# Norm reductions on two PSUM regions, and a broadcast moved by one step, in the attention pairs of a macaron block

## What is computed

```python
# x: (8, 2048, 1024); 16 heads of 64; d_ff 4096, rank 256
x = x + 0.5 * ffn(layernorm(x))          # gelu(P @ V1 + b1) with P = y @ U1, then @ U2 @ V2
x = x + attn(layernorm(x))
x = x + 0.5 * ffn(layernorm(x))

def attn(y):
    q, k, v = (einsum('bpm,hmd->bphd', y, W) + b for W, b in ...)
    logits = einsum('bqhd,bkhd->bhqk', q, k) / sqrt(64)   # causal mask
    return einsum('bqhd,hdm->bqm', einsum('bhqk,bkhd->bqhd', softmax(logits), v), O_w) + O_b
```

## Time and profile before

| | us |
|---|---|
| median of 2 runs | 2237.23 (2233.7 to 2240.76) |
| profiled execution, time | 2229.34 |
| profiled execution, span of the slowest core (core 4) | 2227.6 |
| TensorE busy in that span | 1510.3 (68%) |
| VectorE busy | 569.8 (26%) |
| ScalarE busy | 553.7 (25%) |
| GpSimd busy | 95.0 (4%) |

### The profile page before, as it was taken

One profiled execution on the slowest core, in us unless ns is written; L12 is line 12 of the kernel. 1 busy time (PEld: TensorE's weight loads), 2 busy tenths in 40 slices (PEclk: granted clock), 3 DMA queues, 4 the chain that ended last, 5 costly groups with the idle time before them and its releaser, 6 DMA issues. The chain is left out here.

```text
span 2227.6 us, 17635 instructions; the slowest of 8 cores (2185.7 to 2227.6 us)
## 1 busy us (share of the span) xinstructions
PE 1510.3 (68%) x5571; PEld 415.2 (19%) x5640; DVE 569.8 (26%) x911; ACT 553.7 (25%) x609; POOL 95.0 (4%) x108
## 2 busy tenths in 40 slices
PE   3089997167537586686675876865767578189994
PEld 0022221022112121121121211211211122022221
DVE  3322214442302313114023131131321125312211
ACT  1222231100022232332322323333234201232221
POOL 0100000000100000000000000000100000100000
PEclk9588997588767767576677576767876589599986
DMA  7400000101030100100101101001000102300003
GB/s 223 118 1 1 1 1 14 62 29 62 6 67 0 31 17 10 38 1 10 38 1 29 19 10 38 1 10 29 1 19 0 45 31 71 119 1 1 0 1 151
DMA packets 63652, 72.66 MB, mean 33 GB/s; under 512 B 20390, under 2 KB 51254, under 8 KB 61516
## 3 DMA queue, kind: packets, MB, share of 16 engines
q1 hardware_dynamic: 63564, 71.54, 11.2%
HBM read 50.49 MB, written 12.58 MB: 28 GB/s over the span
## 5 line engine op out<-in xcount | busy, mean ns | idle before, releaser
L668 ACT ACTIVATE pt<-p_big 128x1024 bf16<-128x1024 f32 (+3 forms) x320 | 286.3, 895 | 646.4 <-PE p_big L635 397.0
L629 PE MATMUL p_big<-qgA,kgA 65*128 65x512 bf16 (+3 forms) x320 | 143.8, 449 | 200.8 <-DMA kgB<-u_row 98.9
L531 ACT ACTIVATE hb<-p_big 128x1024 bf16<-128x1024 f32 x128 | 130.7, 1023 | 308.6 <-PE p_big L454 306.7
L452 PE MATMUL p_big<-pb,v1b 128*128 128x512 bf16 x498 | 156.1, 394 | 16.0 <-DVE pb L489 14.9
L590 PE MATMUL p_big<-pt,v_pair 128*64 128x512 bf16 (+3 forms) x320 | 149.9, 469 | 0.0
L593 PE MATMUL p_big<-pt,v_pair 128*64 128x512 bf16 (+3 forms) x320 | 149.5, 467 | 0.0
L635 PE MATMUL p_big<-qgB,kgB 65*128 65x512 bf16 (+3 forms) x320 | 148.6, 464 | 0.0
L586 PE MATMUL p_big<-pt,ones_bf 128*1 128x512 bf16 (+3 forms) x320 | 145.1, 453 | 0.0
L582 PE MATMUL p_big<-pt,ones_bf 128*1 128x512 bf16 (+3 forms) x320 | 138.4, 433 | 0.7
L462 PE MATMUL p_big<-hb,u2b 128*128 128x512 bf16 x502 | 134.4, 389 | 5.9 <-ACT hb L531 4.7
L893 PE MATMUL p_big<-nsq,ones2b 128*1 128x512 bf16 x128 | 51.9, 547 | 81.7 <-DVE u_sc L944 60.0
(11 more groups left out here) (140 smaller groups left out, 1570.9 us busy)
## 6 DMA issues: line engine op xcount, KB each, us to landing
wstage<-u SPq DMA_DIRECT2D x40, 256.0 KB, 4.7
wstage<-v SPq DMA_DIRECT2D x40, 256.0 KB, 4.2
x<-xT SPq DMA_DIRECT2D x8, 1024.0 KB
outT<-x SPq DMA_DIRECT2D x8, 1024.0 KB, 11.0
wstage<-vw SPq DMA_DIRECT2D x16, 256.0 KB
vscr<-vb_s SPq DMA_DIRECT2D x32, 128.0 KB
wst<-qw SPq DMA_DIRECT2D x8, 512.0 KB
wst<-kw SPq DMA_DIRECT2D x8, 512.0 KB
```

Source lines behind the costliest of these rows:

```text
L452: tensor.matmul(psl, v1b[:, rc, 128 * fc:128 * (fc + 1)], pb[:, c % 2, rc, :], start=(rc == 0), stop=False)
L531: ACT.inc(scalar.activation(hb[:, 2 * (fp % 2):2 * (fp % 2) + 2, :], psl.rearrange("p (a b) -> p a b", a=2), AF.Gelu_apprx_tanh))
L629: mm = tensor.matmul(p_big[:, 0:w], kgA[:, ksl], qgA[:, lo:hi], start=True, stop=not first)
L668: ch["XA"].inc(scalar.activation(pt[:, :, i % 2, 0:w], p_big[:, 0:1024].rearrange("p (a b) -> p a b", a=2)[:, :, 0:w], AF.Exp))
```

## The change

1. `emit_bc(c)`, for c = 0, 1, 2, is called at step IC[c]+4 in place of IC[c]+3: 13, 22 and 27.
2. On VectorE, rdbcp(2) and evac(2) stand between round 0 and round 1 of the reductions, no longer behind round 1.
3. Each lane has two rows of PSUM, used by even and odd rounds. Odd rounds use p_big2 columns 0 to 511 (where the projections were) for three lanes, and row 0 of p_big2 columns 1024 to 1535 (where query block 2's output was) for lane (1, 1). So round 1 no longer waits for reductions but for the last copy of the projections (WS) or for evac(2) (DR + 3), and rounds 2 and 3 wait for the reductions of round j-2.
4. The norm matmul (1, 1, 1) is moved from step 26 to step 28.

The number of instructions stays the same on every engine, but for waits.

```diff
@@ the steps of a pair, TensorE @@
-                        c_bc = ICR.get(i - 3)
+                        c_bc = ICR.get(i - 4)
@@ VectorE's order @@
                         aux["dve_red"](vector, 0, 0)
                         aux["dve_red"](vector, 1, 0)
+                    rdbcp(2); evac(2)
+                    if aux:
                         aux["dve_red"](vector, 0, 1)
                         aux["dve_red"](vector, 1, 1)
-                    rdbcp(2); evac(2)
@@ emit_attn_aux_begin @@
-            def nrm_region(which, h):
+            def nrm_region(which, h, j):
                 lane = 2 * which + h
                 if lane < 3:
-                    return p_big2, 32 * lane, 512
-                return p_big, 64, 1024
+                    return p_big2, 32 * lane, (512 if j % 2 == 0 else 0)
+                return (p_big, 64, 1024) if j % 2 == 0 else (p_big2, 0, 1024)
@@ mk_nrm @@
-                    if j >= 1:
-                        tensor.wait_ge(ch["UC"].h, uc_after[(which, j - 1)])
-                    pb, base, coff = nrm_region(which, h)
+                    if in_pair and (which, h) == (1, 1) and j == 1:
+                        tensor.wait_ge(ch["DR"].h, dr0 + 3)
+                    if j == 1 and 2 * which + h < 3:
+                        tensor.wait_ge(ch["WS"].h, ws0 + 10)
+                    if j >= 2:
+                        tensor.wait_ge(ch["UC"].h, uc_after[(which, j - 2)])
+                    pb, base, coff = nrm_region(which, h, j)
@@ the list of items @@
-                items.append((max(26, 24 + 2 * j), ("nrm", 1, 1, j)))
+                items.append((max(26 if j == 0 else 28, 24 + 2 * j), ("nrm", 1, 1, j)))
```

## The result

The changed kernel takes 2184.0 us (median; 2168.4 to 2207.5) beside 2240.2 us for the kernel before, a ratio of 0.9736 (95% interval 0.9698 to 0.9774): 59 us, or 2.6%, faster. The ratio leaves out two runs of the changed kernel (2201.8 and 2207.5 us) that were in a second, slower state with a lower granted clock on one die, so the two medians as they stand differ by 56 us. The forecast was 2162 us in a range of 2140 to 2190. So the direction was right and the time lies in the range, but about 15 us of the 74.5 us forecast are missing. Averaged over repeated runs (59 of the kernel before, 10 of the changed one), the mean span over the eight cores fell from 2223.5 to 2160.1 us and the slowest core's from 2241.4 to 2179.9 us, so it is no effect of one core.

The account below looks back on a forecast made before the run. The prediction took TensorE, with its waits on VectorE's reductions and rdbcp, to bound the attention pairs. Gains of 52 + 8.5 + 11 + 3 = 74.5 us took 2229.3 to 2154.8, or 2162 by the median; range 2140 to 2190.

Parts of the forecast that it names:

- the forecast's own part of it: Whole kernel: the span of times given to the main forecast, 2150 to 2175 us, at a chance of 0.53.
- rival A: TensorE stays at the low clock from step 22 to 39: gain 55 us, 2182 by the median; chance 0.22.
- The stalls and their order: Steps 25 to 28: the 6.95 us wait goes, rdbcp(2)'s falls to about 1 us, nrm(1,1,1) isn't late.
- Where the stall goes: hilo(2) to ScalarE's tail: VectorE's chain becomes the bound, 9.4 us sooner in five pairs, 12.5 in pair 1.
- 59.5 + 8.5: hilo(2) to the tail: 59.5 us gained over pairs 0 to 5, and 8.5 in pair 6.
- The low clock behind the new wait: Steps 36 to 39: TensorE idles behind ScalarE's wait, then runs low, costing 1.5 us in five pairs, 7.5.
- emit_bc: Broadcast one step later covers TensorE's wait for hilo: 1.4 us in 8 pairs, 11, plus 3 in pair 7.
- the clock part: Clock assumptions, to be judged wrong if pairs' stretches before hilo(2) changed by more than 3 us.
- The rule on the clock: From step 25: sustained work would bring the high clock once the 7 us gap goes; the profile row needn't agree.
- rival B: In the pairs, the clock comes up early: gain 98 us, 2131, by the median 2139; chance 0.13.

Follow-up runs that it names:

- e1_bc_only: The kernel before with emit_bc one step later and nothing else: 2242.8 us, ratio 0.9994.
- e7_no_bc_move: The changed kernel with emit_bc back at its old steps (12, 21, 26): 2206.6 us, ratio 0.9823 to the kernel before.

## Why the prediction was right, and where it was not

*The time.* The range held, but the forecast's own part of it, 2150 to 2175, did not: 2184 is the figure of rival A (2182). Its mechanism is not what happened. Rival A had TensorE at the low clock from step 22 to 39 and no wait of ScalarE; in pair 2 the clock was 1.00 from 1028 to 1044, and ScalarE waited in 47 of the 48 pairs 0 to 5 of all cores. Only in pair 5 of core 0 did it not. So that the time is A's is chance, and the mechanism below is the forecast's.

*The stalls and their order.* Right. The waits of 6.95 and 1.25 us went, rdbcp's fell to 1.02, nrm(1, 1, 1) was issued before it was needed, and nothing waited for evac(2).

*Where the stall goes.* Right, and to the microsecond: 27.6 us from hilo(2) to the tail was forecast, 27.3 to 28.7 was measured in pairs 0 to 5 over all cores, with a ScalarE wait of 3.4 to 4.8 us in all but one of them (forecast 2 to 6), and none in pair 6, which took 23.6 on the slowest core (25 taken, 22.9 the lower bound for TensorE). Summed over pairs 0 to 6 this stretch fell by 68.3 us against 59.5 + 8.5 = 68 in the sum.

*The low clock behind the new wait.* The right mechanism, sized too small: 1.5 us a pair in five pairs was taken, and 2.2 measured in most of six (tail to hilo(3) 13.25 in place of 11.03). The term had steps 36 to 39 dearer by at most 0.61 each and by less in the narrow ones; in pair 0 of the slowest core, against pair 2 of the kernel before, step 36 took 0.70 more than at the high clock, step 37 0.81, step 38 0.60, and from step 39 on 0.56, less 0.45 at the tail itself. On the mean over cores 11.3 us in place of 7.5.

*emit_bc.* For c = 0 it gave 1.7 us a pair where 1.4 was taken, and pair 7 in all 4.3 where 3 + 1.4 was. But the prediction adds the move up as if it were independent, and gives emit_bc(2) in pairs 0 to 6 no price. The parts are no sum: alone the move is worth 0 (e1_bc_only), in company some 20 us (e7_no_bc_move), 15 of them between hilo(2) and (3). The sum came out right because the stretch behind hilo(2) was worked out with all parts in place.

*Left out.* hilo(1) to (2) has no term in the sum. It grew by 3.6 us over seven pairs. I had taken the waits there as left unchanged and so as free; they are the place where the clock is lost, at another moment in each pair. The prediction's sign that the clock part is wrong, over 3 us in a stretch ahead of hilo(2), did not come on the mean over cores in any pair (at most 2.9), but single cores had it (39.5 against 45.6 us for one start), in both kernels.

*The missing 15 us.* Against the first profile of before, the mean over cores gives -11.8 + 3.6 - 68.3 + 11.3 + 6.7 - 4.3 = -62.8 us, near the 59 of the timed runs. Against the sum of 74.5 that is 3.8 for the tail, 3.6 for hilo(1) to (2), and 6.7 for the starts, which are mostly scatter between executions (303.8 and 309.1 in two profiles of the same kernel), less 2 for emit_bc in pairs 0 to 7. That names 12 of the 15 us; the rest is the difference between one profile and the timed runs.

*The rule on the clock.* The Trainium skill, "TensorE: Matmul & The Clock Gate" (section "Why this matters for your kernels"), has the clock go down behind long idle gaps and come up with sustained work. The first half agrees with the 4.39 us gap above; yet in pair 1 of core 2 the clock also went down behind a gap of 1.88 us. The second, rival B of the prediction, did not come about: TensorE was busy for all 4 us from 1016 to 1020 and was granted 0.50, and with the 7 us gap gone, pair 2's steps 25 to 27 still ran at the low clock (L629 0.58 to 0.61 us), and it came up only in step 28.

## What to carry to other kernels

When an engine's wait is removed, look along the same engine for the next wait that hangs on the other engine's queue: here, with the broadcast moved alone, what TensorE won ahead of the weight casts (1.8 us in pair 2) came back behind them (2.8 us), until the dependence itself was cut by a second buffer for all four lanes. Parts that are worth nothing alone (0, -1% and 0) can be worth 2.6% together (with two pieces that were not run alone), so test a coupled change whole as well as in pieces. And ask at once what the shortened path hits next: the slack of the side chain (6.85 us) was spent and overdrawn by 4.3 us, and moving one small operation two steps down gave another 2% (2139 us).

## What the runs showed of the hardware

A gain of 33 us in one stretch (14.7 in place of 19.4 us, 7 pairs, all cores) came back in full, nearly all of it in stretches whose instructions were the same, with a lower granted clock (0.756 in place of 0.769 on the mean; 0.55 in place of 0.83 in the one pair shown against its neighbour). In the changed kernel hilo(1) to (2) takes about 15.8, 17.4 or 19.7 to 20.1 us, with 0.95, 0.72 and 0.6 of the clock granted, by where the clock falls. TensorE was also seen busy for 4 us of 4 with 0.50 granted. In a kernel with many short idle times the clock has to be counted over the whole execution and not read from the stretch that was changed.
